# A sort by one-hot ranking on one core: a ring of 35 groups, offsets and totals inside the ranking, placings one iteration later

## The reference, cut to what matters

```
x = x + gnn(layernorm(x), src, dst, edge_weight, ...)      # 12500 nodes, 256 features
x = x + ffn(layernorm(x), ...)                             # 8 experts, the best one of each token
def gnn(x, row, col, vals, ...):                           # 200000 edges
    agg = segment_sum(vals[:, None] * x[col], row)
    h = (1 + eps) * x + agg
    return bn_relu(bn_relu(h @ W1 + b1) @ W2 + b2)
```

## Time and profile before

| | us |
|---|---|
| median of 3 runs | 3261.31 |
| lowest and highest | 3257.73, 3261.65 |
| span of the profiled execution, first to last instruction | 3402.4 |
| of it, the sort block | 0 to about 496 |
| its one-hot tables and ranking | 38.77 to 490.33 |

### The profile page before, as it was taken

How to read it: one execution, slowest core, us unless ns; L and a number is a source line. 1 busy time by engine, 2 the same in 40 slices (tenths; PEclk the granted TensorE clock), 3 DMA queues, 4 the chain that set the end, 5 groups by cost and what they waited for, 6 DMA issues and landing times. The chain is left out here.

```text
span 3402.4 us, 70209 instructions
## 1 busy us (share of the span) xinstructions
PE 2886.5 (85%) x20200; PEld 2410.0 (71%) x20201; DVE 2419.2 (71%) x5921; ACT 1668.3 (49%) x3267; POOL 747.4 (22%) x733
## 2 busy tenths in 40 slices
PE   4676668888888886999999999977989989679998
PEld 2232337777777776888888888755767767479998
DVE  8887547777777775888888888766565666666665
ACT  3564346666666664222222222675666666543332
POOL 1000005555555554000000000031121121212222
PEclk9998559999999998999999999998999999889999
DMA  2332017777777777999999999101334343466664
GB/s 42 110 112 71 1 37 265 300 277 288 291 291 292 293 292 283 332 334 331 328 340 341 328 340 327 27 0 36 132 138 160 143 155 139 179 216 211 214 211 145
DMA packets 214806, 710.52 MB, mean 209 GB/s; under 512 B 28495, under 2 KB 104313, under 8 KB 189514
## 3 DMA queue, kind: packets, MB, share of 16 engines
q1 hardware_dynamic: 130778, 405.55, 34.6%
q0 software_dynamic: 83952, 304.02, 23.0%
HBM read 383.91 MB, written 340.05 MB: 213 GB/s over the span
## 5 line engine op out<-in xcount | busy, mean ns | idle before, releaser
L1337 PE MATMUL coll_ps_sum<-coll_rows,coll_hot 128*128 128x256 f32 x2940 | 658.6, 381 | 23.9 <-DVE coll_hot L1272 23.3
L988 PE MATMUL send_ps_msg<-send_parts,send_pick 128*128 128x256 f32 x3584 | 555.6, 299 | 110.6 <-ACT send_msg L1028 98.4
L1337 PEld LDWEIGHTS coll_ps_sum<-coll_rows,coll_hot 128*128 128x128 f32 x2940 | 550.6, 191 | 102.4 <-DVE coll_hot L1272 27.5
L988 PEld LDWEIGHTS send_ps_msg<-send_parts,send_pick 128*128 128x128 f32 x3584 | 472.6, 197 | 132.1 <-issue 64.6
L1028 ACT ACTIVATE send_msg<-send_ps_msg 128x1024 f32<-128x1024 f32 x448 | 454.3, 1027 | 215.8 <-PE send_ps_msg L988 190.5
L843 POOL DMA_INDIRECT messages<-send_msg,send_to x448 | 476.7, 1064 | 367.4 <-ACT send_msg L1028 224.0
L891 DVE TENSOR_SCALAR send_pick<-send_ps_local,edges_down 128x512 fp32r<-128x512 f32 x448 | 334.4, 747 | 201.2 <-PE send_ps_local L976 161.1
L1272 DVE TENSOR_SCALAR coll_hot<-coll_nodes,coll_rows 128x128 f32<-128x128 f32 x1470 | 393.6, 341 | 4.7 <-issue 1.9
L1391 ACT ACTIVATE nodes_hid<-coll_ps_turned 128x256 f32 (+1 forms) x98 | 37.6, 384 | 552.3 <-PE coll_ps_turned L1169 552.3
L1934 DVE TENSOR_TENSOR gate_act_lo<-gate_act_h,gate_act_hi 128x512 fp32r<-128x512 f32 x200 | 140.6, 703 | 171.2 <-ACT gate_act_hi L1843 160.6
L2390 PE MATMUL exp_ps_y<-exp_w_hi,exp_hT_hi 128*128 x840 | 244.5, 291 | 6.2 <-DVE exp_hT_lo L2344 6.2
(11 more groups left out here) (322 smaller groups left out, 5858.9 us busy)
## 6 DMA issues: line engine op xcount, KB each, us to landing
coll_rows<-messages SPq DMA_DIRECT2D x98, 1300.0 KB, 7.4
coll_rows<-messages SPq DMA_DIRECT2D x98, 1170.0 KB, 7.5
exp_pay<-regions SPq DMA_DIRECT2D x105, 646.0 KB
send_window<-node_rows SPq DMA_DIRECT2D x112, 128.0 KB
node_rows<-sort_xn SPq DMA_DIRECT2D x25, 512.0 KB, 5.0
coll_own<-node_rows SPq DMA_DIRECT2D x98, 128.0 KB, 4.1
sort_xt<-in_x_dram SPq DMA_DIRECT2D x24, 512.0 KB, 4.4
layers_w<-in_x_dram SPq DMA_DIRECT2D x24, 384.0 KB
```

Source lines behind the costliest of these rows:

```text
L988: ins = pe.matmul(ps_msg[:, q % 2, a, :], pick[:, q * RUN + a, :], parts[:, s % 2, part, :], start=(part == 0), stop=(part == 1))
L1337: ins = pe.matmul(ps_sum[:, s, 0:D], hot_of(s, j), features(u, j), start=(j == CX), stop=(j == CJ - 1))
```

## The change

The ring `hot` has 35 slots in place of 28, so tables and counts run 35 groups ahead of the ranking, and 7 tables are made before the first rank. Since the counts of the next batch are then complete at the 21st group of the running one, `offsets` is split into `needs` and `offsets`, called on DVE in iterations 21 and 22 of each batch for the next one, and on PE between the two halves of the ranks 22 and 23 (`needs`, `firsts`). `offset` has two buffers, and the small products use the unused corner `scratch` of the last PSUM bank of `ranks`. `totals` is cut into six steps, one in each of the iterations 79 to 84, in the PSUM of `counts`. In the last batch the four placings of an iteration are done one iteration later on PE, with 4 buffers in place of 2; half of the tables are written by DVE (two of each four, with the values -0.5 and 0.5, for which `moves` is doubled) and half by ACT. Some work areas move into memory of the ring.

The diff, cut to its core (PE's `totals` is cut into five functions with the same matmuls, written to `counts`):

```diff
 BATCH = 28
+RING = 35
...
-        hot = m.sb("hot", [P, BATCH, T2, NB, 2], BF16)
+        hot = m.sb("hot", [P, RING, T2, NB, 2], BF16)
...
-        offset = m.sb("offset", [P, T2, NB, 2], F16)
+        offset = m.sb("offset", [P, 2, T2, NB, 2], F16)
...
-        reached = m.sb("reached", [NB, 2, RUNS], BF16)
-        dest = m.sb("dest", [P, NG, QS])
+        reached = m.sb("reached", [NB, 4, RUNS], BF16)
...
+        dest = raw[:, 0:2 * NG * QS].bitcast(F32).rearrange("p (g q) -> p g q", q=QS)
+        of_run = raw[:, 16 * GE + 2 * BATCH * P:16 * GE + 2 * BATCH * P + 2 * RUNS].bitcast(I32)
...
+        NEEDS_AT = 2 * BATCH - RING
+        TOTALS_AT = (NBATCH - 2) * BATCH + NEEDS_AT + 2
+        PUTS_AT = NG - NG // 4
+        scratch = ranks[:, 6:8].rearrange("p a f -> p (a f)")[:, PITCH:2 * PITCH]
...
-                def reach(i, s):
-                    if later(i, 2):
-                        act.wait_ge(placed, i - 1)
-                    act.activation(reached[:, s, :], k.of_run[0:NB, :], ACT.Sign, bias=edge[:, i:i + 1]).then_inc(reached_ready, 1)
+                def reach(i):
+                    if i >= 4:
+                        act.wait_ge(placed, i - 3)
+                    act.activation(reached[:, i % 4, :], k.of_run[0:NB, :], ACT.Sign, bias=edge[:, i:i + 1]).then_inc(signs_ready, 1)
                 act.wait_ge(asked, 6)
-                for n in range(NG):
-                    reach(n, n % 2)
+                for n in range(0, NG, 4):
+                    reach(n)
+                    reach(n + 1)
...
-                    if n >= BATCH:
-                        dve.wait_ge(ranked, 2 * (n - BATCH + 1))
-                    dve.tensor_tensor(hot[:, n % BATCH], k.bucket_pairs(n).unsqueeze(2).to_broadcast([P, T2, NB, 2]),
+                    if n >= RING:
+                        dve.wait_ge(ranked, 2 * (n - RING + 1))
+                    dve.tensor_tensor(hot[:, n % RING], k.bucket_pairs(n).unsqueeze(2).to_broadcast([P, T2, NB, 2]),
...
-                def offsets(b):
+                def needs(b):
                     steps.restart()
-                    mine = slice(b * BATCH, (b + 1) * BATCH)
                     dve.wait_ge(counted, (b + 1) * BATCH)
-                    steps.link(dve.tensor_copy(tiles[:].rearrange("g a b u -> g a (b u)"), counts[0:BATCH, 0:T2, 0:2 * NB]))
+                    dve.tensor_copy(tiles[:].rearrange("g a b u -> g a (b u)"), counts[0:BATCH, 0:T2, 0:2 * NB]).then_inc(counts_copied, 1)
+                    dve.wait_ge(counts_copied, b + 1)
...
-                    dve.tensor_copy(runs[:, mine], ranks[0:NB, 0, 0:BATCH]).then_inc(runs_ready, 1)
+                    dve.tensor_copy(runs[:, b * BATCH:(b + 1) * BATCH], scratch[0:NB, 0:BATCH]).then_inc(runs_ready, 1)
+                def offsets(b):
                     dve.wait_ge(first_done, b + 1)
-                    dve.tensor_copy(k.first[:, mine], ranks[0:NB, 4, 0:BATCH])
-                    steps.link(dve.tensor_scalar(base[:], ranks[0:BATCH, 2, 0:NB], float(RUN), 1.0 - SCALE, ALU.mult, ALU.add))
+                    if b >= 2:
+                        dve.wait_ge(ranked, 2 * (b - 1) * BATCH)
+                    steps.link(dve.tensor_scalar(base[:], scratch[0:BATCH, P:P + NB], float(RUN), 1.0 - SCALE, ALU.mult, ALU.add))
+                    dve.tensor_copy(k.first[:, b * BATCH:(b + 1) * BATCH], scratch[0:NB, 0:BATCH]).then_inc(first_kept, 1)
                     steps.link(dve.tensor_tensor(pairs[:], upto[:, 0:T2, :], base[:].unsqueeze(1).to_broadcast([BATCH, T2, NB]), ALU.add))
-                    dve.tensor_copy(offset[0:BATCH, :, :, 0], pairs[:])
-                    dve.tensor_tensor(offset[0:BATCH, :, :, 1], pairs[:], tiles[:, :, :, 0], ALU.add).then_inc(offset_ready, 1)
+                    dve.tensor_copy(offset[0:BATCH, b % 2, :, :, 0], pairs[:])
+                    dve.tensor_tensor(offset[0:BATCH, b % 2, :, :, 1], pairs[:], tiles[:, :, :, 0], ALU.add).then_inc(offset_ready, 1)
...
-                def totals():
+                def asks():
                     steps.restart()
+                    dve.wait_ge(first_kept, NBATCH)
...
+                    by_four = moves[:].rearrange("b (g r) v -> b g r v", r=4)
+                    steps.link(dve.tensor_scalar(by_four[:, :, 2:4, :], by_four[:, :, 2:4, :], 2.0, None, ALU.mult))
...
+                def reach(i):
+                    if i >= 4:
+                        dve.wait_ge(placed, i - 3)
+                    dve.tensor_scalar(reached[:, i % 4, :], k.of_run[0:NB, :], k.first[:, i:i + 1], -0.5,
+                                      ALU.is_ge, ALU.add).then_inc(halves_ready, 1)
...
                 dve.wait_ge(col_kept, 1)
                 for n in range(BATCH):
                     buckets(n)
-                for b in range(NBATCH):
-                    offsets(b)
-                    if b == NBATCH - 1:
-                        totals()
-                    for n in range(b * BATCH, (b + 1) * BATCH):
-                        highest(n)
-                        if n + BATCH < NG:
-                            buckets(n + BATCH)
-                    slots(b)
+                needs(0)
+                offsets(0)
+                for n in range(BATCH, RING):
+                    buckets(n)
+                total_steps = (asks, turned_runs, earlier_runs, starts, moved_starts, raise_flag)
+                for n in range(NG):
+                    b, l = divmod(n, BATCH)
+                    highest(n)
+                    if n + RING < NG:
+                        buckets(n + RING)
+                    if b + 1 < NBATCH:
+                        if l == NEEDS_AT:
+                            needs(b + 1)
+                        if l == NEEDS_AT + 1:
+                            offsets(b + 1)
+                    if TOTALS_AT <= n < TOTALS_AT + len(total_steps):
+                        total_steps[n - TOTALS_AT]()
+                    if n >= PUTS_AT:
+                        reach(4 * (n - PUTS_AT) + 2)
+                        reach(4 * (n - PUTS_AT) + 3)
+                    if l == BATCH - 1:
+                        slots(b)
...
+                    if g == 0 and n > 0:
+                        pe.wait_ge(counts_copied, n // BATCH)
...
+                def firsts(b):
                     mine = slice(b * BATCH, (b + 1) * BATCH)
-                    pe.wait_ge(need_ready, b + 1)
-                    pe.matmul(ranks[0:NB, 0, 0:BATCH], need[:], c.ident[0:BATCH, 0:BATCH], start=True, stop=True).then_inc(need_turned, 1)
                     pe.wait_ge(runs_ready, b + 1)
-                    pe.matmul(ranks[0:BATCH, 2, 0:NB], runs[:, mine], k.below[0:NB, 0:NB], start=True, stop=True)
-                    pe.matmul(ranks[0:NB, 4, 0:BATCH], k.below[0:NB, 0:NB], runs[:, mine], start=True, stop=True).then_inc(first_done, 1)
+                    pe.matmul(scratch[0:BATCH, P:P + NB], runs[:, mine], k.below[0:NB, 0:NB], start=True, stop=True)
+                    pe.matmul(scratch[0:NB, 0:BATCH], k.below[0:NB, 0:NB], runs[:, mine], start=True, stop=True).then_inc(first_done, 1)
+                    pe.wait_ge(first_kept, b + 1)
                 def rank(n):
-                    g = n % BATCH
+                    b, g = divmod(n, BATCH)
                     for h, (a0, a1) in enumerate(HALVES):
                         if n > 0:
                             pe.wait_ge(reduced, 2 * n + h - 1)
+                        if h == 1 and b + 1 < NBATCH:
+                            if g == NEEDS_AT + 1:
+                                needs(b + 1)
+                            if g == NEEDS_AT + 2:
+                                firsts(b + 1)
...
+                def put(i):
+                    if i == 0:
+                        pe.wait_ge(asked, 6)
+                    by_sign = i % 4 < 2
+                    pe.wait_ge(signs_ready if by_sign else halves_ready, i // 4 * 2 + i % 2 + 1)
...
+                needs(0)
+                firsts(0)
+                for n in range(BATCH, RING):
+                    count(n)
+                total_steps = (turn_runs, sum_earlier, sum_totals, take_changes, find_bad)
+                for n in range(NG):
+                    rank(n)
+                    if n >= 1 and n - 1 + RING < NG:
+                        count(n - 1 + RING)
+                    if TOTALS_AT <= n < TOTALS_AT + len(total_steps):
+                        total_steps[n - TOTALS_AT]()
+                    if n > PUTS_AT:
+                        for i in range(4 * (n - PUTS_AT - 1), 4 * (n - PUTS_AT)):
+                            put(i)
+                for i in range(NG - 4, NG):
+                    put(i)
```

84 lines of the change are left out of this document (41 added, 43 removed).

## The result

| us | changed kernel | kernel before |
|---|---|---|
| median (4 runs each) | 3207.77 | 3261.48 |
| lowest and highest | 3201.47, 3209.26 | 3257.73, 3262.46 |
| ratio, 95% interval | 0.9839, 0.9827 to 0.9851 | |
| end of the sort in the profile | 444.91 | 496.28 |

The change takes 53.7 us off, 1.6%. I had said 3235 us and a range of 3211 to 3248: the sign was right, and the gain is twice the forecast and outside the range. Measured again among the experiments, it gave 3207.48 us and a ratio of 0.984 (0.9827 to 0.9854).

What follows compares the result with a forecast made beforehand. In the last batch no engine was full, so engines waited for each other. The four parts summed as +0.3 - 2.4 + 4.8 - 28.8 = -26 us, from a median of 3261.3 to 3235 us, range 3211 to 3248.

Steps and rivals of the forecast that it cites:

- The clock: Last batch: PE likelier stays at half clock despite having no idle time, at 3.09 us an iteration; forecast chance 0.52.
- rival (a): Last batch: the clock rises, DVE bounds at 2.34 us an iteration; total -46 us, 3215 us; chance 0.33.
- The DVE table: Last batch: each new 99x512 scalar operation on DVE takes 0.39 us, with 0.22 and 0.75 as ends.
- Placings: Last batch: 16 weight loads and matmuls of placings on PE at 0.06 us each, 0.96 us an iteration.
- Part 1: Seven tables before the first rank: early layer-norm calls wait 8.9 us, savings elsewhere nearly offset them; sum +0.3 us.
- Part 2: Offsets inside the ranking: old waits of 8.0 us go, new product waits cost 5.6; sum -2.4 us.
- Part 3: Totals inside the ranking: five round-trip waits of 11.2 us replace 7.3 of waits and gaps; sum +4.8 us.
- (b): Last batch: a handover is left in the placings, 3.4 to 3.8 us an iteration; total -6.5 to -18; chance 0.06.
- (c): Last batch: PE waits for DVE's tables, 4.85 us an iteration; total +21 us, 3283 us; chance 0.04.
- (d): ACT stays pace-setter, or round trips and early layer norm cost twice the sum; what remains within 6.5 us; chance 0.05.
- part 4: Placings: last batch at 3.09 us an iteration, bound by PE at half clock, 86.3 us against 115.1; gain 28.8.

Runs made afterwards that it cites:

- e9_slower_dve: Changed kernel with DVE writing four further tables that nobody reads in each last-batch iteration; 3406.8 us (one run), kernel before 3423.21.
- e1: Changed kernel with the placings as before: two buffers, all tables on ACT, placings in their own iteration; 3262.13 us, ratio 1.0012 to the kernel before.
- e5: Changed kernel with each group's placings back right after its own rank, four buffers and DVE's share kept; 3418.57 us, ratio 0.9987 to the kernel before.
- e2: Kernel before with only the new placings: four buffers, half the tables on DVE, placings one iteration later; 3205.74 us, ratio 0.9836.
- e3: Kernel before with four table buffers in place of two and nothing else; 3219.78 us, ratio 0.9874.
- e12: Kernel before with the new placings and the layer norm's scales one group after means in place of two; 3174.97 us, ratio 0.9741.
- e4: Changed kernel with ACT writing all tables, four buffers and placings one iteration later kept; 3220.03 us, ratio 0.9878 to the kernel before.
- e6: Changed kernel with no layer norm in the seven early tables and scales one group after means; 3340.03 us, ratio 0.9770 to the kernel before.
- e7: Changed kernel with the five products of the totals queued on PE behind the next rank, not ahead; 3359.65 us, ratio 0.9823 to the kernel before.

## Why the prediction was wrong

**The clock: the step that failed.** The prediction said of the last batch: "I hold it for likelier that this does not lift the clock". That was the step. Its reasoning set 79% busy of PE for over 100 us at 1.2 GHz beside an iteration of 3.09 us in which 0.96 are placings of four columns, and took the share of ranks in the iteration as what counts. After the change PE had no gap from 380 to 386 us, and the clock rose in the third iteration, to 1.00 for the rest of the batch. The evidence for that stood in the same group of rows, 2.00 of 2.00 us busy at batch 1 and then the rise, and I gave it a chance of 0.33. e9_slower_dve shows what keeps it down: the same placings and ranks, with one wait of 0.84 us in each iteration, stay at 0.50 for 95 us. Whether it is the wait itself or the smaller share of ranks that comes with it stays open; the forecast's own share, 2.13 of 3.09 us, was lower than the real one, 2.13 of 2.74, because its placings were too dear (below). The sentence against rival (a), "DVE would then leave PE gaps again", was right about the gaps (PE is busy 1.70 of 2.00 us after the rise) and wrong about what follows: once at 2.4 GHz, PE kept that with waits of 0.2 to 0.4 us. The rows of before had this too: in the ranking the clock is 0.96 with PE busy for 61.68 of 84.00 us, a smaller share than the 79% on which the forecast stayed at 1.2 GHz. The Trainium skill, "TensorE: Matmul & The Clock Gate", Part 1, says that the throttled clock is the default and that activity of PE releases it. The rise in the changed kernel agrees: PE was busy without a gap from 379.74 us, and the clock was at 2.4 GHz before 386.

In time: the forecast's batch was 86.3 us, the measured one 59.6. By the prediction's own sums the clock is 20.2 of these 26.7 (86.3 to rival (a)'s 66.1). By measured durations it is less: an iteration at 1.2 GHz took 2.74 us (381.27 to 384.01) and not 3.09, so a whole batch at that clock would have been about 2.6 + 27 x 2.74 = 76.6 us (an estimate), and the clock is 17.0.

**The DVE table: a term too large.** The other 6.5 us of the prediction's sums are DVE's new operation. I took 0.39 for 99x512, nearest by length to a conversion from int32. Measured were 0.344 for one and 0.26 from start to start (0.60 for two, with 0.52 from 429.45 to 429.97). So the iteration is 1.57 + 0.52 = 2.09 and not 2.34, and 27 x 0.25 is 6.8 us. Both ends, 0.22 and 0.75, were written down, but used only for the half clock, where they change nothing. In rival (a), where DVE bounds, the lower end gives 1.56 + 0.44 = 2.00 us an iteration, 27 x 0.34 = 9 us less, and 3206 in place of 3215. A range that reached there would have held the result; mine ended at 3211 and missed it by 3 us. The Trainium skill, "VectorE: DVE Perf Modes", section "The perf-mode tier table", gives `tensor_scalar` and `tensor_copy` on bfloat16 in SBUF a faster mode than on float32. The trace agrees in direction: one operation from float16 to bfloat16 took 0.344 us, against 0.42 for the conversion of nearly the same length from int32. No run here has the same operation in both widths.

**Placings: another term too large.** I doubled the 0.48 us of 8 weight loads to 0.96 for 16. But 16 weight loads took 0.69 us at 1.2 GHz (381.86), and their matmuls 0.61; at 2.4 GHz the matmuls took 0.54 (430.11). At the half clock, where PE bounds, that is 27 x 0.35 = 9.5 us too much in the forecast, which should have read about 3225. At the clock that came it didn't matter, since DVE bounds.

**Part 1 was right.** The seven early calls waited 2.18, 2.94, 0.90 and 2.94 us, where 2.14, 2.95, 0.86 and 2.95 stood, and the first reduction came without a wait (86.65). L537 waited 21 times in place of L528's 24: two waits went from the ranking, two came in the early tables, and three are hidden by `offsets`, `needs` and `slots`.

**Part 2 was right in the mean.** Waits for the products of 6.0 us in four batches, the one at the first batch 1.15, the last 1.48, the longest 1.8, where 1.7 and 1.6 stood; a half rank of 0.39 where 0.2 stood.

**Part 3 had one wait too many.** 2.17, 2.11, 2.50 and 1.20 us are 8.0, where five waits of 11.2 stood. Three have the predicted size. By the fourth the clock had risen (1.00 from 368 us on), and it is 1.20 where 2.07 stood. The fifth isn't there: `slots(2)` stands on DVE between step and reduction (375.30 to 378.67) and gives PE its time. That is visible in the order of the code, `l == BATCH - 1` after `total_steps`, and I hadn't followed it. Parts 1 to 3 together were +2.7 by the sum and +3.8 in e1. With part 3's waits 3.2 us under their term the sum should have been about -0.5; which term makes up for it isn't shown, and 2 us of it can be the difference of two profiles. That the totals agree so well is luck in part.

**The rivals.** (a) is what happened, in mechanism and nearly in size: -46 forecast and -51.4 in the sort; the DVE table alone, 6.8 us, is more than the difference. (b) and (c) did not happen, because the tables are one iteration ahead; e5 shows what they would have been, 3.99 us an iteration, just under the 4.05 from which (c) decides. (d) fell with e1 and e2.

**What part 4 consists of** was only half seen. The prediction had the cause in its first paragraph ("two wait for ACT, which had its buffers freed only at 456.03"), but the sum of part 4 gives the gain to tables that are shared and early, and no term to the buffers. e3 shows that the two further buffers alone bring 44.0 us, and the sharing with the delay 11.2 more.

## What to carry to other kernels

Where PE stands at 1.2 GHz for a long stretch with short waits in every iteration, price a removed wait twice: by the wait, and by the ranks at the other clock, and let the range reach to the ends of the unknown durations in that case too. Look for the cheapest edit that takes the wait away: here two more buffers gave most of it, and three of the four written parts gave nothing. When an engine becomes the bound, read all its waits again: the largest here, 36.7 us for the layer norm, was in the profile of before, and one character took most of it away.

## What the runs showed that I had not expected

The same ranks and placings ran for a whole batch at either clock, and what another engine did decided. PE stayed at 1.2 GHz for 95 us and more where it had waits in each iteration at that clock: 0.71 and 0.35 us of 4.11 in before, 0.93 of 3.99 in e5, 0.76 of 3.65 in e9. Where it had none at 1.2 GHz the clock rose within the first iterations, and then stayed at 2.4 GHz to the end with waits of 0.2 to 0.4 us (after, e2, e12). In e3 and e4, where ACT bounds, it went up and down.

The chips differ by 5% on this kernel. The kernel before took 3259 to 3261 us beside eight of the runs and 3423 on the chip that e5, e6, e7 and e9 ran on. Busy time in the next stage, after the sort, of before, of e5 and of after:

```profile
700.00:900.00 200.00, 169.48 (x1668) 155.56 (x1669) 144.25 (x297) 125.02 (x215) 115.50 (x107) 0.94 0.75 286
```

```profile
520.00:1300.00 780.00, 657.92 (x6557) 597.62 (x6556) 554.74 (x1144) 485.20 (x833) 437.55 (x417) 0.96 0.75 287
```

```profile
650.00:850.00 200.00, 196.85 (x2083) 180.33 (x2083) 178.97 (x364) 156.71 (x265) 159.78 (x133) 1.00 0.93 354
```

The last two figures of each line are the share of the DMA engines' time and GB/s: 0.75 and 286 or 287 on the slow one, 0.93 and 354 otherwise. So the profile of before shows what e5's chip shows (0.75, 0.74, 0.76 and 0.75 from 700 to 900 us in the four profiles on it, and 0.93 in the nine others, all with the same code there). The text ahead of the prediction puts the 141 us between span and median down to the recording. That is not so: the profiled run of every other kernel here lies within 7 us of its median, but for e6's (14 us). The slower transfers account for it (the stage took 824 us against 669), and that this profile was taken on such a chip is likely, though nothing on record names it. What makes these transfers slower wasn't tried. The sort doesn't feel it: in the profiles of like kernels DVE received PE's product in the last `needs` at 346.49 to 347.88 us on the slow chip and at 347.08 to 348.63 on the others.
